# Pairwise tower with embedding lookups: one-hot lookups in every stage, smaller batches of sums, another order of events

## The reference, cut to what matters

```python
# 1024 rows, 32 fields, embeddings of 64; tables of 1000 to 125000 rows
e = stack([tbl_f[ids[:, f]] for f in range(32)], axis=1)          # 1024 x 32 x 64
p, q = e[:, ROW], e[:, COL]                                       # 496 pairs of fields
kp = einsum('bpj,ipj->bpi', p, kernel)                            # 64 x 64 matrix for each pair
z = sum(kp * q, axis=-1)                                          # 1024 x 496
h = concatenate([z, dense_ctx], axis=1)                           # 16 dense features
h = maximum(h @ W_top1 + b_top1, 0)                               # 512
h = maximum(h @ W_top2 + b_top2, 0)                               # 256
y = h @ W_top3
```

## Time and profile before

| what | us |
| --- | --- |
| median of 3 runs | 451.96 (451.67 to 453.82) |
| the profiled execution, its time | 451.3 |
| its span, first to last instruction | 449.5 |
| TensorE busy with matmuls | 428.2 (95%) |
| TensorE busy with weight loads, beside the matmuls | 283.0 (63%) |
| VectorE busy | 302.9 (67%) |
| ScalarE busy | 70.5 (16%) |
| GpSimd busy | 230.5 (51%) |

### The profile page before, as it was taken

The page is one execution under the profiler, slowest core; times in us unless marked ns, Lnnn a source line. Parts: engine busy times, 40 slices in busy tenths (PEclk is TensorE's granted clock), DMA queues, the critical chain, the costliest instruction groups (busy, mean ns, idle before and its releaser), DMA issues.

```text
span 449.5 us, 10096 instructions
## 1 busy us (share of the span) xinstructions
PE 428.2 (95%) x4290; PEld 283.0 (63%) x4290; DVE 302.9 (67%) x324; ACT 70.5 (16%) x154; POOL 230.5 (51%) x248
## 2 busy tenths in 40 slices
PE   0769999999999999999999999999999999999997
PEld 0447666767676766767676676767676766664442
DVE  4466687786878686886788787877887787860000
ACT  1002211102021111011221110111211201101122
POOL 4775776556576656565767574747674300000000
PEclk9989999999999999999999999999999999999999
DMA  5663444342111111110111110111151000000000
GB/s 141 199 192 80 126 123 125 100 131 62 22 40 39 25 33 25 20 41 18 39 36 30 29 28 19 39 23 37 31 177 33 14 1 14 1 1 1 0 0 0
DMA packets 15316, 23.55 MB, mean 52 GB/s; under 512 B 5505, under 2 KB 7809, under 8 KB 15144
## 3 DMA queue, kind: packets, MB, share of 16 engines
q1 hardware_dynamic: 6884, 14.14, 10.4%
q0 software_dynamic: 7808, 8.01, 9.3%
q10 hardware_dynamic: 580, 0.76, 0.6%
HBM read 20.79 MB, written 0.00 MB: 46 GB/s over the span
## 4 chain that ended last, share of the span: by engine, by line
PE 95%; DMA 3%; issue 1%; ACT 0%; SPq 0%
PE kp L535 52%; PE z_ps L552 25%; PE kp L573 6%; PE tr_ps L519 5%; PE tr_ps L511 3%; PE kp L579 3%; DMA k_sb<-in_tbl 3%; PE kp L586 0%; ACT pair L393 0%; ACT prod L437 0%; SPq L332 0%; SPq L338 0%; SPq L341 0%
## 5 line engine op out<-in xcount | busy, mean ns | idle before, releaser
L481 DVE TENSOR_TENSOR prod<-kp,pair 128x1024 f32<-128x1024 f32 x224 | 259.0, 1216 | 83.9 <-PE kp L535 83.9
L375 POOL DMA_INDIRECT raw<-in_tbl,ids_sb x244 | 230.3, 944 | 122.1 <-issue 67.0
L535 PE MATMUL kp<-pair,k_sb 64*128 64x256 f32 x1984 | 238.8, 387 | 0.0
L535 PEld LDWEIGHTS kp<-pair,k_sb 64*128 64x128 f32 x1984 | 182.9, 187 | 41.9 <-DVE prod L481 11.3
L552 PE MATMUL z_ps<-prod,ones_sel 128*32 128x256 f32 x1984 | 117.0, 382 | 0.0
L552 PEld LDWEIGHTS z_ps<-prod,ones_sel 128*32 128x32 f32 x1984 | 59.7, 110 | 50.5 <-issue 10.7
L393 ACT ACTIVATE pair<-tr_ps 128x256 f32<-128x256 f32 x64 | 24.5, 383 | 247.4 <-PE tr_ps L519 218.6
L511 PE MATMUL tr_ps<-prod,k_sb 125*64 125x256 f32 x96 | 14.3, 464 | 17.9 <-DMA k_sb<-in_tbl 13.4
L491 DVE TENSOR_TENSOR prod<-kp,pair 128x512 f32<-128x512 f32 x48 | 30.0, 681 | 0.0
L573 PE MATMUL kp<-z_sb,k_sb 128*128 128x512 f32 x64 | 28.0, 596 | 0.0
L519 PEld LDWEIGHTS tr_ps<-ident,raw 128*128 128x128 f32 x122 | 12.3, 141 | 24.2 <-issue 23.3
(11 more groups left out here) (9 smaller groups left out, 7.4 us busy)
## 6 DMA issues: line engine op xcount, KB each, us to landing
k_sb<-in_kd SPq DMA_DIRECT2D x15, 512.0 KB, 4.1
raw<-in_tbl,ids_sb POOLq DMA_INDIRECT x244
pair<-pair SPq DMA_DIRECT2D x32, 64.0 KB, 2.3
k_sb<-in_tbl SPq DMA_DIRECT2D x6, 250.0 KB
k_sb<-in_w SPq DMA_DIRECT2D x1, 1024.0 KB
hot_ids_sb<-in_hot_ids SPq DMA_DIRECT2D x3, 250.0 KB
z_sb<-in_dense ACTq DMA_DIRECT2D x1, 512.0 KB, 8.8
k_sb<-in_w SPq DMA_DIRECT2D x1, 512.0 KB
```

What stands on the lines that cost most here:

```text
L375: nc.gpsimd.indirect_dma_start(raw[:, r % RAW_RING, i, n, :], None, tables[f], bass.IndirectOffsetOnAxis(ap=ids_sb[:, 2 * b + i, f:f + 1], ...
L481: nc.vector.tensor_tensor(prod[:, u % PROD_RING, :, :].rearrange("p q (i n) -> p (q i) n", i=UNIT_SLOTS), kp[u % KP_RING][:, :, :].rearran ...
L535: last = nc.tensor.matmul(kp[u % KP_RING][:, q, i * WIDTH:(i + 1) * WIDTH], k_sb[rows, x, :], pair[rows, group_place(st, owner // 2), :], ...
```

## The change

What it does:

- Ten lookups in place of three. The first stage has four (groups 0, 2, 4 and 6), each later stage has two (groups 2 and 6), with one-hots made behind given units of the stage before or of the same stage (`hot_units`, `hots_behind`), in a buffer of their own, `hot_sb`. Gathers fall from 61 groups to 54.
- The small tables are padded on the host to 1024 rows in an array `small` of their own and loaded over all 128 partitions, one DMA for each lookup. The two that the later stages use are loaded a second time at unit 24 into `late_table_sb`.
- One comparison covers both fields (512 columns) where two covered 256 each.
- The ids come in two pieces, the first stage's first; the dense features are loaded at unit 24 from SP instead of at the start from ScalarE's queue.
- Batches are four units (the last of a stage two), a sum stands behind the third unit of the next batch (LAG 3), and `prod` has 8 places where it had 12.
- TRANSPOSE_AT is written anew: in most places one event right behind each sum.

The MLP, the products, VectorE's products and the mixing are unchanged. The diff, cut to its core:

```diff
 KP_RING = 3
-PROD_RING = 12
-LAG = 4
+PROD_RING = 8
+LAG = 3
 RAW_RING = 4
...
 STAGES_PER_HALF = ROWS // WIDTH
-BATCH_UNITS = (5, 6, 5)
+BATCH_UNITS = (4, 4, 4, 4)
...
-LOOKUP = (0, 2, 4)
-SMALL = 1000
-SMALL_P, SMALL_C = 125, 8
+LOOKUP = ((0, 0), (0, 2), (0, 4), (0, 6), (1, 2), (1, 6), (2, 2), (2, 6), (3, 2), (3, 6))
+EARLY = 4
+SMALL_GROUPS = tuple(k for st, k in LOOKUP[:EARLY])
+LATE_GROUPS = tuple(k for st, k in LOOKUP[EARLY:EARLY + 2])
+assert all(LOOKUP[i][1] == LATE_GROUPS[i % 2] for i in range(EARLY, len(LOOKUP)))
+SMALL, SMALL_C = 1000, 8
 HOT_UNITS = 2 * SMALL_C * WIDTH // (2 * ROWS)
+DENSE_AT = 24
 UNIT_SLOTS = ROWS // WIDTH
...
             first = len(gathers)
-            if st or k not in LOOKUP:
+            if (st, k) not in LOOKUP:
                 gathers += [(g, st) for g in range(k, k + n)]
...
     st, k, n, raws = EVENT[e]
-    return LOOKUP.index(k) if st == 0 and k in LOOKUP else None
+    return LOOKUP.index((st, k)) if (st, k) in LOOKUP else None
 def group_event(st, k):
...
-TRANSPOSE_AT = [0, 0, 0, 1, 2, 3, 7, 9, 13, 15, 20, 23, 25, 31, 36, 41, 43, 47, 52, 57, 61, 62, 66, 71, 74, 77, 82,
-                87, 90, 93, 98, 103, 105, 109, 114, 119, 123, 124, 128, 133, 136, 139, 144, 149, 152, 155, 160, 165,
-                167, 171, 176, 181, 185, 186, 190, 195, 198, 201, 206, 211, 214, 217, 222, 227]
+TRANSPOSE_AT = [0, 0, 0, 1, 2, 4, 7, 10, 11, 17, 23, 27, 31, 39, 43, 47, 51, 55, 62, 63, 64, 66, 69, 72, 73, 79, 85,
+                89, 93, 101, 105, 109, 113, 117, 124, 125, 126, 128, 131, 134, 135, 141, 147, 151, 155, 163, 167,
+                171, 175, 179, 186, 187, 188, 190, 193, 196, 197, 203, 209, 213, 217, 225, 229, 233]
 assert len(TRANSPOSE_AT) == len(EVENT)
...
            for u in range(UNITS) for s in unit_slots(u) for tile in SLOT[s] for g in groups_of(tile))
+def look_event(i):
+    return group_event(*LOOKUP[i])
+def hot_units(i):
+    end = TRANSPOSE_AT[look_event(i)] - 1
+    first = max(end - 2 * SMALL_C, TRANSPOSE_AT[look_event(i - 1)] + 1)
+    return [first + c * (end - first) // SMALL_C for c in range(SMALL_C)]
+def hots_behind(u):
+    return [(i, c) for i in range(EARLY, len(LOOKUP)) for c, at in enumerate(hot_units(i)) if at == u]
 def events_at(u):
...
         w3_sb = sb("w3_sb", [P, N2, 32])
-        hot_ids_sb = sb("hot_ids_sb", [P, len(LOOKUP), 2, WIDTH], I32)
+        hot_ids_sb = sb("hot_ids_sb", [P, EARLY, 2 * WIDTH], I32)
+        hot_sb = sb("hot_sb", [P, SMALL_C, 2 * WIDTH])
+        late_table_sb = sb("late_table_sb", [P, len(LATE_GROUPS), 2, SMALL_C, EMBED])
         row_sb = sb("row_sb", [P, SMALL_C])
...
-        T_SLOTS = len(LOOKUP) * 2 * SMALL_C * EMBED // P
-        table_sb = k_sb[:, SLOTS - T_SLOTS:SLOTS, :].rearrange("p a n -> p (a n)").rearrange(
-            "p (i n c e) -> p i n c e", i=len(LOOKUP), n=2, c=SMALL_C)
-        def hot(i, n, c):
-            at = (SMALL_C * n + c) * WIDTH
-            return prod[0:SMALL_P, HOT_UNITS * i + at // (2 * ROWS), at // ROWS % 2, at % ROWS:at % ROWS + WIDTH]
+        T_SLOTS = EARLY * 2 * SMALL_C * EMBED // P
+        early_table_sb = k_sb[:, SLOTS - T_SLOTS:SLOTS, :].rearrange("p a n -> p (a n)").rearrange(
+            "p (i n c e) -> p i n c e", i=EARLY, n=2, c=SMALL_C)
+        def table(i, n, c):
+            return early_table_sb[:, i, n, c, :] if i < EARLY else late_table_sb[:, i % 2, n, c, :]
+        def hot(i, c):
+            if i < 2:
+                return prod[:, HOT_UNITS * i + c // 2, c % 2, :]
+            if i == 3:
+                return z_sb[:, c // 2, c % 2 * ROWS:(c % 2 + 1) * ROWS]
+            return hot_sb[:, c, :]
         W_SLOTS = (FC * HID1 + N1 * HID2) // P
...
         ids_in = sem("ids_in")
+        ids_rest_in = sem("ids_rest_in")
         consts_in = sem("consts_in")
         row_no_in = sem("row_no_in")
-        hot_ids_in = [sem(f"hot_ids_in{i}") for i in range(len(LOOKUP))]
-        table_in = [sem(f"table_in{i}") for i in range(len(LOOKUP))]
+        hot_ids_in = [sem(f"hot_ids_in{i}") for i in range(EARLY)]
+        table_in = [sem(f"table_in{i}") for i in range(EARLY)]
+        late_tables_in = sem("late_tables_in")
         hot_ready = sem("hot_ready")
...
             def load_hot_ids(i):
-                sp.dma_start(hot_ids_sb[0:SMALL_P, i, :, :],
-                             hot_ids[i:i + 1, :, :].broadcast_to([SMALL_P, 2, WIDTH])).then_inc(hot_ids_in[i], 16)
+                sp.dma_start(hot_ids_sb[:, i % EARLY, :],
+                             hot_ids[i:i + 1, :].broadcast_to([P, 2 * WIDTH])).then_inc(hot_ids_in[i % EARLY], 16)
             def load_tables(i):
-                for n in range(2):
-                    table = tables[2 * LOOKUP[i] + n].rearrange("(p c) e -> p c e", c=SMALL_C)
-                    sp.dma_start(table_sb[0:SMALL_P, i, n, :, :], table).then_inc(table_in[i], 16)
+                sp.dma_start(early_table_sb[:, i, :, :, :], small[:, i, :, :, :]).then_inc(table_in[i], 16)
             load_hot_ids(0)
-            sp.dma_start(row_sb[0:SMALL_P, :], row_no).then_inc(row_no_in, 16)
+            sp.dma_start(row_sb[:, :], row_no).then_inc(row_no_in, 16)
             load_tables(0)
...
             load_tables(2)
-            for j in range(1, K_AHEAD):
+            load_k(1)
+            load_hot_ids(3)
+            load_tables(3)
+            for j in range(2, K_AHEAD):
                 load_k(j)
...
                     mix_across(st, m)
+                for i in range(EARLY, len(LOOKUP)):
+                    if u == hot_units(i)[0] - 6:
+                        sp.wait_ge(hot_ready, SMALL_C * (i - EARLY + 1))
+                        sp.wait_ge(kp_done, u + 1)
+                        load_hot_ids(i)
+                if u == DENSE_AT:
+                    sp.wait_ge(kp_done, u + 1)
+                    sp.dma_start(z_sb[:, FC - 1, :], dense).then_inc(dense_in, 16)
+                    for n, k in enumerate(LATE_GROUPS):
+                        sp.dma_start(late_table_sb[:, n, :, :, :],
+                                     small[:, SMALL_GROUPS.index(k), :, :, :]).then_inc(late_tables_in, 16)
                 j = s // K_LOAD
...
             for r, (g, b) in enumerate(GATHER):
+                if b and not GATHER[r - 1][1]:
+                    pool.wait_ge(ids_rest_in, 16)
                 if r >= RAW_RING and EVENT_OF[r - RAW_RING] != (EVENT_OF[r - RAW_RING - 1] if r > RAW_RING else None):
...
         def _(act):
-            act.dma_start(ids_sb[:, :, :], ids).then_inc(ids_in, 16)
+            act.dma_start(ids_sb[:, 0:WIDTH // P, :], ids[:, 0:WIDTH // P, :]).then_inc(ids_in, 16)
             act.dma_start(ident[:, :], ident_in).then_inc(consts_in, 16)
             act.dma_start(ones_sel[:, :], sel_in).then_inc(consts_in, 16)
-            act.dma_start(z_sb[:, FC - 1, :], dense).then_inc(dense_in, 16)
+            act.dma_start(ids_sb[:, WIDTH // P:, :], ids[:, WIDTH // P:, :]).then_inc(ids_rest_in, 16)
             def evacuate(e):
...
                             dve.wait_ge(mixed_in[m % MIX1_RING], 16 * (mixed_use(st, m) + 1))
+            def make_hot(i, c):
+                if c == 0:
+                    dve.wait_ge(hot_ids_in[i % EARLY], (i // EARLY + 1) * 16)
+                    if i >= EARLY:
+                        dve.wait_ge(transposed, look_event(i - 1 if i > EARLY else 2) + 1)
+                nc.vector.tensor_scalar(hot(i, c), hot_ids_sb[:, i % EARLY, :], row_sb[:, c:c + 1], None,
+                                        ALU.is_equal).then_inc(hot_ready, 1)
             dve.wait_ge(row_no_in, 16)
-            for i in range(len(LOOKUP)):
-                dve.wait_ge(hot_ids_in[i], 16)
+            for i in range(EARLY):
                 for c in range(SMALL_C):
-                    for n in range(2):
-                        nc.vector.tensor_scalar(hot(i, n, c), hot_ids_sb[0:SMALL_P, i, n, :],
-                                                row_sb[0:SMALL_P, c:c + 1], None,
-                                                ALU.is_equal).then_inc(hot_ready, 1)
+                    make_hot(i, c)
             for u in range(UNITS):
...
                 if u < PROD_RING and u % HOT_UNITS == 0:
-                    dve.wait_ge(transposed, group_event(0, LOOKUP[u // HOT_UNITS]) + 1)
+                    dve.wait_ge(transposed, look_event(u // HOT_UNITS) + 1)
                 if st and u == summed_behind(chunk_end(st - 1, FC - 1)) + 1:
...
                     last.then_inc(prod_done, 1)
+                for i, c in hots_behind(u):
+                    make_hot(i, c)
             add_dense(LAST)
...
                 if lookup is not None:
-                    pe.wait_ge(table_in[lookup], 2 * 16)
+                    if lookup < EARLY:
+                        pe.wait_ge(table_in[lookup], 16)
+                    else:
+                        pe.wait_ge(late_tables_in, len(LATE_GROUPS) * 16)
                     for c in range(SMALL_C):
+                        pe.wait_ge(hot_ready, SMALL_C * lookup + c + 1)
```

(20 more changed lines are left out.)

5 lines of the change are left out of this document (3 added, 2 removed).

## The result

The changed kernel takes 469.6 us (median of 4 runs, 467.85 to 470.93) against 451.8 for the kernel before (4 runs, 450.11 to 453.82): a ratio of 1.039 [1.033, 1.044]. The profiled execution took 469.4. The forecast was 463.3 with a range up to 469: the sign was right; the profiled execution took 6.1 more than forecast, and the median lies 0.6 beyond the range.

What follows compares the result with a forecast made beforehand. TensorE was taken as the bound (95% of the chain). From 451.3 us: +17.4 loop, +2.1 VectorE stall, -7.1 start, -0.4 tail = 463.3; range 459 to 469, with 0.76 on 459 to 466.

Steps and rivals of the forecast that it cites:

- The loop: Unit 7 to the last loop sum: 377.9 us, 17.4 more than before; six late lookups add 19.6.
- The stall of VectorE: Stages 1 to 3: TensorE waits 0.7 us each for the second late lookup's comparisons, +2.1; bounds 0 and about 13.6.
- The start: Up to unit 7: it starts at 34.0, not 41.1, saving 7.1 us, with VectorE binding; bounds 33.2 and 36.
- TensorE's own chain: Before unit 7: first lookup at 6.5, second 13.4, unit 0 at 17.0, third lookup ended 23.2; ahead of VectorE.
- Row numbers and constants: At the start: inputs to VectorE's first comparisons, taken as ready at 4.6 us, between 3.8 and 6.5.
- Rival 1: Late lookups and one at unit 7 run at the sums' rate, 1.88 us each: 451.0, not slower; chance 0.07.
- Rival 2: The start gives nothing because the fourth ids land late: unit 7 near 41, 470.4 us; chance 0.09.
- Rival 3: VectorE becomes the bound where comparisons stand: 467 to 472 us; chance 0.08.
- Rival 4: The promised absence of rests between gathers fails: GpSimd's 50.6 us of rests grow; no time changes, no chance given.
- The tail: Behind the loop: the last sum has two units, not three, -0.4 us.

Runs made afterwards that it cites:

- s2_after: The changed kernel run again without edits, beside the kernel before on the same undisturbed chip: 465.64 us, ratio 1.032.
- e5_batches_and_events: The kernel before with only the batches of four, LAG 3 and the new TRANSPOSE_AT, on a chip with late instructions: ratio 1.0008.
- f1: The changed kernel with VectorE's later comparisons and SP's later loads both held until the first gathered block landed: 467.03 us, ratio 1.0354.
- f2_halves: The changed kernel with each 512-column comparison split into two of 256 columns: 465.61 us, ratio 1.0318.
- e3_vector_pause: The changed kernel with VectorE waiting for the first gathered block before the second lookup's comparisons: 527.49 us beside a before of 528.2, ratio 0.998.
- V: Not a run but a theory the experiments tested: VectorE's long train of 512-column comparisons holds GpSimd's gather instructions.
- e2: The changed kernel with SP's loads after the first two lookups' held until the first gathered block landed: 525.37 us beside a before of 528.2, ratio 0.998.
- D: Not a run but a theory the experiments tested: SP's loads fill the sixteen DMA engines, and the first gathered block comes late among them.
- e8: The changed kernel without its six late lookups and fourth early one, gathers in their place, beside a before of 530.4 us: ratio 1.020.
- e9: As e8, with the third ids loaded earlier and SP's loads released in steps behind the first and second gathered blocks: ratio 1.023.

## Why the prediction was wrong in size and right in sign

- **The loop held.** Unit 7 to the MLP was to take 377.9 + 2.1; it took 377.74 (42.55 to 420.29), 0.4 of stalls included, and 377.72 in s2_after. Six late lookups for six transposes, 18 more ends of runs, no stalls of fifth units: each price was within 0.03 us. This stretch is 17.1 us longer than before; 17.4 were forecast without the stalls.
- **The stall of VectorE, +2.1, was mis-sized.** I took 0.57 for a comparison of 512 columns, from 1.04 ns for each added column, which is what VectorE's products show. Measured: (6.52 - 0.48) / 15 = 0.40 for 512 columns, and 0.26 for 256 where no gather runs beside them (e5_batches_and_events), so 256 more columns cost 0.14, or 0.55 ns each. The 0.30 that I took as the base was itself stretched by gathers. The stall was 0.27 - 0.14 = 0.13 a stage. The Trainium skill, VectorE: DVE Perf Modes, section "The perf-mode tier table", gives float32 `tensor_scalar` twice the rate of `tensor_tensor` from SBUF. The traces agree, for comparisons with an int32 input: 0.55 ns for an added column against 1.04.
- **The start, -7.1, was the failed step.** Unit 7 came at 42.55, not 34.0. That is +8.6; with -2.3 in loop and stall it gives 6.3, and 469.4 - 463.3 is 6.1. The two misses have opposite signs, so the total looks better than its terms. I had named VectorE as what binds the start, ending its comparisons at 22.7. They ended at 18.8, since each took 0.40, and the order of who is last turned over.
- **Why the block was not there.** TensorE's own chain, which I had at unit 0 by 17.0, took it for granted that the first gathered block is there after the first lookup. "No row has TensorE waiting for a gather" was true of before, where the first lookup ran from 13.40 to 18.7 and would have hidden a late block. The change removed that cover, and I didn't ask when the block would come then. By an estimate, losing the cover alone would have cost next to nothing. Counted in packets (6912 for 216 gathers in after, so 32 each), GpSimd's queue in before had moved four gathers' worth, 128, by 12.9, and after's first lookup ended at 13.07. What failed is that I let the loads and comparisons change and left the block where it was.
- **What the late block cost.** Unit 0 came at 25.9, not 17.0: 0.85 from TensorE's later begin (7.35 for 6.5), 5.31 of waiting, and 2.8 for a lookup at the lower clock (6.46 against 3.67), in sum 9.0. From there to unit 7 it took 16.65, TensorE's own work; by that, unit 0 at 17.0 would have meant unit 7 at 33.7 (an estimate), so the 34.0 would have come out nearly right though VectorE wasn't what binds. No run got there: f1 had unit 0 at 18.51 and unit 7 at 38.80.
- **Both causes of the late block are side effects of parts that I had counted as gains.** Loads on sixteen engines, as forecast, meant 99.7% of them busy from 10.4 to 15.6 where 59.5% had been, and a block that comes 4.6 to 5.0 us after its last gather instruction instead of 1.5: shown by f2_halves and e3_vector_pause with V away, by e2 and f1 with D away. One comparison for two fields meant 512 columns, beside which an ordinary gather instruction takes 1.28 for 0.94: shown by f2_halves. In the first trace the long hold came on top and decided the last part: the fourth gather ended at 15.61, the block landed 2.6 later, while in s2_after, with D and no long hold, TensorE had it at 16.18. e8 and e9, where a held gather alone put the block at 18.2, show the same. Fewer bytes ahead of the first gather, or another event order on TensorE, were not tried.
- **Row numbers and constants**: 5.80, within the 3.8 to 6.5 that I allowed, though not the 4.6 that I took; it cost nothing, as VectorE wasn't last. `ones_sel` let TensorE begin at 7.35, not 6.5.
- **Rival 1** fell: lookups take 3.60. **Rival 2** gave nearly its time (470.4) by another cause: its ids were not late. Had I asked of each input of the start whether it could be late, its 0.09 would have been larger, and the range would have reached it. **Rival 3** fell with the 0.40. **Rival 4** was right, and as forecast changed nothing: rests 50.6 to 105.6 us.
- **The tail**: 47.3 from the start of the MLP to the end against 47.8, as the -0.4 said.

## What to carry to other kernels

A wait that isn't in the profile may be covered by another wait that the change removes, and the change may also move it: for each input that TensorE reads in the part you shorten, work out when it will be ready with the new loads and the new neighbours, and from which queue. Loads spread over all the DMA engines came sooner here, but what was small and urgent and went through another queue then came later, and holding the loads back only moved the wait. A lookup by matmul costs TensorE ten times a transpose (3.60 against 0.37), so where TensorE is the bound and GpSimd rests, it pays only where it shortens a wait.
